# The run mask and the last factors of a graph network's last pass move to PSUM bank 7, its product groups to banks 0 to 6

## What is computed

```python
# he: edge_attr_16, rel_type: edge_type_90
V = weight.reshape(in_dim, num_bases, out_dim)
W_rel = jnp.matmul(w_comp, V).reshape(num_rels, in_dim, out_dim)
h_src = h[src]
z_src = h_src @ Ws.T
z_dst = h[dst] @ Ws.T
z_e = he @ Ws.T
e = jnp.concatenate([z_src, z_e, z_dst], axis=1) @ Wa.T
msg = jnp.einsum('ei,eio->eo', h_src, W_rel[rel_type]) * e
h_out = jax.ops.segment_sum(msg, dst, num_segments=n_nodes)
```

## Time and profile before

| what | value |
|---|---|
| median of 3 runs | 16045.7 us |
| lowest and highest | 16036.34 and 16046.12 us |
| span of the profiled execution | 16080.2 us |
| busy: PE, DVE, ACT, POOL | 77%, 79%, 50%, 74% |
| chain that ended last, by line | L637 on POOL 54% |
| mean granted clock of TensorE | 0.848 |

### The profile page before, as it was taken

How to read it: one execution, slowest core, us unless ns; L and a number is a source line. 1 busy time by engine, 2 the same in 40 slices (tenths; PEclk the granted TensorE clock), 3 DMA queues, 4 the chain that set the end, 5 groups by cost and what they waited for, 6 DMA issues and landing times.

```text
span 16080.2 us, 197886 instructions
## 1 busy us (share of the span) xinstructions
PE 12414.4 (77%) x62964; PEld 11204.4 (70%) x62964; DVE 12672.3 (79%) x13275; ACT 8008.6 (50%) x6941; POOL 11959.0 (74%) x12266
## 2 busy tenths in 40 slices
PE   6777777777599999599999488888888377777774
PEld 5555555555599998599999377777777376766764
DVE  7777777777577777477777589899989599999996
ACT  1111111111466666466666377777777255555552
POOL 6777777777777777677777677777777577777776
PEclk8888888888799999799999688898888577777776
DMA  1111111111122221122221122222222222222221
GB/s 37 28 27 27 28 28 27 28 28 26 33 40 39 40 39 37 28 40 39 40 39 38 37 48 50 50 51 50 50 47 48 44 61 62 63 60 63 61 62 37
DMA packets 811074, 675.53 MB, mean 42 GB/s; under 512 B 420924, under 2 KB 729500, under 8 KB 810500
## 3 DMA queue, kind: packets, MB, share of 16 engines
q1 hardware_dynamic: 419012, 545.90, 11.4%
q0 software_dynamic: 392000, 128.94, 9.3%
HBM read 507.78 MB, written 166.09 MB: 42 GB/s over the span
## 4 chain that ended last, share of the span: by engine, by line
POOL 57%; issue 20%; DVE 8%; DVEq 8%; PE 6%; DMA 1%; ACT 0%; POOLq 0%; SPq 0%; ACTq 0%
POOL deep L637 54%; DVE big L1292 6%; PE PS L855 5%; DVEq L1040 4%; DVEq L1297 3%; POOL deep L646 3%; DVE sml L1561 0%; DVEq L1232 0%; DVE acc L1229 0%; DMA wgt<-in_edge_weight 0%; DVEq L1286 0%; DVE sml L1553 0%; DVE acc L1566 0%; DVE sml L1554 0%; DVE sml L1558 0%
## 5 line engine op out<-in xcount | busy, mean ns | idle before, releaser
L637 POOL DMA_INDIRECT deep<-table,idx x11750 | 11475.0, 977 | 3824.8 <-issue 3579.0
L797 PE MATMUL PS<-tparts,hot 125*128 125x400 f32 x22000 | 4163.7, 350 | 482.7 <-DVE big L1451 305.4
L797 PEld LDWEIGHTS PS<-tparts,hot 125*128 125x128 f32 x22000 | 4078.7, 192 | 567.4 <-DVE big L1451 387.1
L1292 DVE TENSOR_TENSOR big<-PS,deep 128x768 f32<-128x768 f32 (+4 forms) x2750 | 2984.7, 1085 | 1082.2 <-DMA deep<-table,idx 515.5
L855 PE MATMUL PS<-tparts,rhot 125*128 125x426 f32 (+1 forms) x9000 | 2302.2, 428 | 527.7 <-DVE big L1292 293.8
L855 PEld LDWEIGHTS PS<-tparts,rhot 125*128 125x128 f32 x9000 | 2177.8, 246 | 616.3 <-DVE big L1292 320.7
L944 ACT ACTIVATE hot<-deep,ones_col 128x1536 fp32r<-128x1536 bf16 x1000 | 1447.6, 1472 | 1464.7 <-PE PS L797 1424.8
L754 PE MATMUL PS<-w0b_sb,big 128*128 128x256 f32 x6250 | 1826.1, 437 | 428.4 <-DVE big L1292 390.1
L754 PEld LDWEIGHTS PS<-w0b_sb,big 128*128 128x128 f32 x6250 | 1342.2, 222 | 933.7 <-DVE big L1292 475.0
L869 PE MATMUL PS<-wx,hot 115*128 115x272 f32 x12500 | 1726.1, 293 | 311.1 <-DVE big L1292 311.1
L1275 DVE TENSOR_REDUCE acc<-big 128x64 f32<-128x1024 f32 (+2 forms) x1875 | 1940.6, 1035 | 18.3
(11 more groups left out here) (281 smaller groups left out, 9713.7 us busy)
## 6 DMA issues: line engine op xcount, KB each, us to landing
wide<-edge_types SPq DMA_DIRECT2D x250, 800.0 KB, 6.1
deep<-table,idx POOLq DMA_INDIRECT x11750, 2.4
wide<-pick_codes SPq DMA_DIRECT2D x250, 352.0 KB, 3.5
running<-msg SPq DMA_DIRECT2D x250, 212.5 KB, 2.1
running<-msg SPq DMA_DIRECT2D x250, 200.0 KB, 2.0
running<-msg SPq DMA_DIRECT2D x125, 400.0 KB, 2.5
wide<-in_edge_attr SPq DMA_DIRECT2D x125, 200.0 KB, 2.5
tabo<-pick_codes SPq DMA_DIRECT2D x125, 160.0 KB, 4.6
```

The source lines that it names most:

```text
L637: pool.indirect_dma_start(g[:, j, 0:GW[l]], None, tab_dram[l][:, :], bass.IndirectOffsetOnAxis(ap=idx[:, s, j:j + 1], axis=0)).then_inc(ga ...
L797: last = pe.matmul(o, poneh[0:NQ, m, c], tparts[0:NQ, k, m * JC:m * JC + JC], start=m == 0 and k == 0, stop=m == BK - 1 and k == 1)
L1292: dve.tensor_tensor(products(j), matv(l, j, n), xs, ALU.mult).then_inc(mats_free, 1)
```

## The change

What the diff does:

- **Pass 4's mask** stands in PSUM bank 7 in f32, columns 0 to 415, as one buffer 16 features wide. Both scans read it there. ACT writes it (400 elements) when the scans of the chunk before are done (`scanned`); before, it asked for `chunks_done`. The zeros of its first column are written once ahead of the pass.
- **Pass 4's factor** goes to bank 7 as well (`fac_ps`, columns 420 to 444), and the multiplication that was L1650 reads it there. Since DVE now writes to bank 7 where ACT writes the mask, DVE waits for the mask (`masked`) ahead of the factor's sum and no longer ahead of the scans.
- **Pass 4's groups** get banks 0 to 6 alone: the three slots (4,3), (0,2), (2,2), then (4,2), (0,2), (2,2) and so on. Before, the groups stood at (0,3), (3,2), (5,2), (0,2), (2,2), (4,2), (6,2), (3,2), (7,1). Each group now waits for the group three before it. Before, that was 5, 3, 5, 3, 3, 3, 4, 2 and 2 before it, in the groups' order.
- **Passes 1 and 2**: ACT writes the mask of a chunk ahead of its one-hot vectors instead of behind them, and DVE waits for the mask at the chunk's start instead of ahead of the scan. Their scan goes over 442 elements instead of 416, because its length now comes from `FLATC`.
- A new event `banks_set` lets ACT start each of the passes 1, 2 and 4 only when DVE has set up bank 7.

```diff
-             [(0, 3), (3, 2), (5, 2), (0, 2), (2, 2), (4, 2), (6, 2), (3, 2), (7, 1)]]
+             [(4, 3), (0, 2), (2, 2), (4, 2), (0, 2), (2, 2), (4, 2), (0, 2), (2, 1)]]
...
-        def maskv(s):
-            return mask[:, HOME[s], :].rearrange("p (c t) -> p c t", t=CH + 1)
+        MASK_BANK = [[None] * 5] * 4 + [[7] * 5]
+        FLATC = [17, 17, 17, 17, 16]
+        def mask_flat(l, s):
+            n, b = FLATC[l] * (CH + 1), MASK_BANK[l][s]
+            return mask[:, HOME[s], 0:n] if b is None else PS[:, b, 0:n]
+        def maskv(l, s):
+            return mask_flat(l, s).rearrange("p (c t) -> p c t", t=CH + 1)
+        fac_ps = PS[:, 7, 420:420 + CH]
...
             def run_mask(l, it, s):
-                act.wait_ge(chunks_done, it * S + (NCH * l + s + S - 1))
-                act.activation(maskv(s)[:, :, 1:CH + 1], bc_r(same[:, bass.ds(it * (S * CH) + CH * s, CH)], 17),
+                if l == 4:
+                    act.wait_ge(scanned, it * S + (NCH + s))
+                else:
+                    act.wait_ge(chunks_done, it * S + (NCH * l + s + S - 1))
+                act.activation(maskv(l, s)[:, :, 1:CH + 1], bc_r(same[:, bass.ds(it * (S * CH) + CH * s, CH)], FLATC[l]),
                                ACT.Identity).then_inc(masked, 1)
...
                         act.wait_ge(rows_in[s], it * 16 + (row_base(l) + 16))
+                        run_mask(l, it, s)
                         code = rows_h[:, HOME[s], :]
...
-                        run_mask(l, it, s)
                         act.drain()
...
             def scans(l, it, s):
                 W = CW[l]
-                dve.wait_ge(masked, it * S + (NCH * l + s + 1))
-                for c0 in range(0, W, 17 if W == 17 else C):
-                    n = min(17 if W == 17 else C, W - c0) * (CH + 1)
-                    a = acc[:, HOME[s], c0 * (CH + 1):c0 * (CH + 1) + n]
-                    last = dve.tensor_tensor_scan(a, mask[:, HOME[s], 0:n], a, 0.0, ALU.mult, ALU.add)
+                if l in (0, 3):
+                    dve.wait_ge(masked, it * S + (NCH * l + s + 1))
+                n = FLATC[l] * (CH + 1)
+                for c0 in range(0, W * (CH + 1), n):
+                    a = acc[:, HOME[s], c0:c0 + n]
+                    last = dve.tensor_tensor_scan(a, mask_flat(l, s), a, 0.0, ALU.mult, ALU.add)
...
                         chunk_in(l, it, s)
-                        nodes_of_bank(l, it, s, iota_jr)
+                        dve.wait_ge(masked, it * S + (NCH * l + s + 1))
+                        nodes_of_bank(l, it, s, iota_jr(l, s))
...
             table_parts(4)
+            dve.memset(maskv(4, 0)[:, :, 0], 0.0)
+            dve.drain()
+            dve.sem_inc(ev["banks_set"], 1)
...
                         if i == 1:
-                            dve.tensor_tensor(sml[:, 1, :], term[:, s, :], gatv(s, 4)[:, :, C], ALU.add)
+                            dve.wait_ge(masked, it * S + (NCH * 4 + s + 1))
+                            dve.tensor_tensor(fac_ps, term[:, s, :], gatv(s, 4)[:, :, C], ALU.add)
                     matrices(4, it, s, C, whole_term)
-                    then(dve.tensor_tensor(m[:, :, 0:C], m[:, :, C:2 * C], bc_c(sml[:, 1, :]), ALU.mult))
+                    then(dve.tensor_tensor(m[:, :, 0:C], m[:, :, C:2 * C], bc_c(fac_ps), ALU.mult))
                     scans(4, it, s)
```

More of the change, by code:

```diff
@@ L46 @@
     "lp_tanh", "agg_n2", "agg_n",
-] + ["ln_in", "ln_out"] \
+] + ["ln_in", "ln_out", "banks_set"] \
   + ["tab", "strad_in", "strad_out", "strad_used", "out_ready"]
@@ L349, in accv, with iota_jr @@
             return acc[:, HOME[s], 0:CW[l] * (CH + 1)].rearrange("p (c t) -> p t c", t=CH + 1)
-        def maskv(s):
-            return mask[:, HOME[s], :].rearrange("p (c t) -> p c t", t=CH + 1)
+        MASK_BANK = [[None] * 5] * 4 + [[7] * 5]
[5 more added lines that the diff above has]
+            return mask_flat(l, s).rearrange("p (c t) -> p c t", t=CH + 1)
+        def iota_jr(l, s):
+            return iota_jr_ps if l in (1, 2) else iota_f[:, 0:JR]
+        iota_jr_ps = PS[:, 7, 512 - JR:512]
+        fac_ps = PS[:, 7, 420:420 + CH]
         def nodes(a, w=C):
@@ L365, in build_gnn @@
         iota_ps = PS[:, 7, P:2 * P]
-        iota_jr = PS[:, 7, 512 - JR:512]
         block = ctx.enter_context(nc.Block())
@@ L932, in pick_digits @@
                 y = PICKED.index(l)
+                act.wait_ge(ev["banks_set"], l)
                 with act.Fori(0, IT) as it:
@@ L1024, in _ @@
             root_of("ln_in", na[0:NQ, 3, :], na[0:NQ, 2, :], "ln_out", 3)
+            act.wait_ge(ev["banks_set"], 3)
             for s in range(S):
@@ L1437, in gcn_pass @@
                 y = PICKED.index(l)
-                then(dve.tensor_copy(iota_jr, iota_f[:, 0:JR]))
+                dve.tensor_copy(iota_jr_ps, iota_f[:, 0:JR])
+                dve.drain()
+                dve.sem_inc(ev["banks_set"], 1)
                 def pick_sum(s, i):
@@ L1459, in gcn_pass @@
                         columns_in(l, it, s, 0)
-                        then(dve.tensor_tensor(accv(s, l)[:, 1:CH + 1, :], gatv(s, l),
-                                               wgt[:, s, :].unsqueeze(2).to_broadcast([P, CH, C]), ALU.mult))
+                        then(dve.tensor_tensor(accv(s, l)[:, 1:CH + 1, :], gatv(s, l), bc_c(wgt[:, s, :]), ALU.mult))
                         scans(l, it, s)
@@ L1573, in hyper_chunk @@
                 chunk_in(3, it, s)
-                nodes_of_bank(3, it, s, iota_f[:, 0:JR])
+                nodes_of_bank(3, it, s, iota_jr(3, s))
                 matrices(3, it, s, 0, amid)
@@ L1641, in _ @@
                     chunk_in(4, it, s)
-                    nodes_of_bank(4, it, s, iota_f[:, 0:JR])
+                    nodes_of_bank(4, it, s, iota_jr(4, s))
                     sums_free(4, it, s)
```

## The result

| | median | runs |
|---|---|---|
| before | 16046.12 us | 7 (16036.34 to 16053.72) |
| changed | 16002.71 us | 7 (15995.96 to 16014.25) |
| ratio | 0.9973 | 95% interval 0.9962 to 0.9983 |

The change saves 43 us in this comparison; the interval reaches from 27 to 61 us. The forecast was 53 us less, 15993 us, with a range of 15972 to 16025.

What follows compares the result with a forecast made beforehand. POOL's source-row fetches, stretched by DVE in pass 4, were taken to bound the kernel, with DVE next. The terms 46.6 + 3.5 + 4 - 1 = 53 us, from 16045.7, gave 15993 us, range 15972 to 16025.

Steps and rivals of the forecast that it cites:

- The mechanism: Pass 4: DVE instructions with two SBUF inputs stretch POOL's fetches; one input in PSUM removes the stretch of 87.5 us.
- The rival in which the fetches are not freed: Pass 4: the scan's remaining SBUF accesses hold the lock, POOL stays at 25.74 us a chunk, time 16046; chance 0.07.
- The cap: Pass 4: of the 87.5 us stretch only the 46.6 us that DVE waits for fetched rows shows in the end.
- DVE's pace: Pass 4: DVE sets the pace once fetches are freed, at 25.31 us a chunk, above POOL's 25.03.
- The multiplication: Pass 4, L1650: 963 to 935 ns, 3.5 us gained; the mask's wait leaving the gap before the scan, 4 us.
- Scans from PSUM: Pass 4's scans reading f32 from PSUM cost 0 us, as PSUM is not dearer.
- The rival with the slower scan: Pass 4: each scan from PSUM takes 0.42 us more, DVE's pace is 26.16 us a chunk, time 16099; chance 0.07.
- the one with a dearer start: Pass 4: a PSUM input adds 0.07 us to each of three DVE instructions, 26 us lost, time 16019; chance 0.13.
- My own argument from L1254: L1254's 275 elements from PSUM (445 ns) and 125 from SBUF (292 ns) give 1.02 ns an element, 164 ns a start.
- The ring: Pass 4's new bank order: picks start some 0.6 us earlier; 0 us, with a gain of up to 7.3 us.
- Passes 1 and 2: ACT's `Abs` come 6.5 us later, covered by about 1.7 us: 0 us; the longer scan costs 1 us.
- The rival in which this comes too late: Passes 1 and 2: the `Abs` use up the cover; each further 0.2 us costs 50 us, time 16043; chance 0.04.

Runs made afterwards that it cites:

- each half alone: The changed kernel with only the scans reading PSUM (factor back in SBUF), or only the multiplication (mask back in SBUF): ratios to before 0.9966 and 0.9967.
- a_again: The changed kernel, unedited, timed and profiled once more beside the kernel before: 16001.97 us against 16052.72, ratio 0.9969.
- the second profile of before: The kernel before, unedited, profiled once more: span 16053.3 us; timed against itself, ratio 1.0.
- e2_factor_in_sbuf: The changed kernel with pass 4's factor back in SBUF, so only the scans read an input from PSUM: ratio to before 0.9966.
- e3_mask_in_sbuf: The changed kernel with pass 4's mask back in SBUF as bf16, so only the multiplication reads an input from PSUM: ratio to before 0.9967.
- the first experiment: The kernel before with only pass 4's groups moved to banks 0 to 6 in three slots, mask and factor staying in SBUF: ratio 1.0.

## Why the prediction was right, point by point

- **The mechanism.** Forecast: with one input in PSUM, the two scans and the multiplication no longer stretch fetches. Shown by the mean of 944 ns and by each half alone taking away half. The rival in which the fetches are not freed is out. More exactly than I wrote, only an instruction that is already running when the fetch starts holds it up.
- **The cap.** Forecast: only the 46.6 us that DVE waited show, not all of the stretch. Shown by those waits gone, by the two runs with more work on DVE (42 us on the changed kernel, none before), and by the one with less (46 us of 121).
- **DVE's pace.** Forecast 25.31 us a chunk. The copy's first and last start in the changed kernel (`a_again`) give (15834.3 - 12690.5) / 124 = 25.35, and in before (15889.7 - 12695.8) / 124 = 25.76. For pass 4 my terms made 54 us and my sign was 50 to 58 us; it is 49.9 and 49.8, just below that. The first pair of profiles, place by place on DVE over 124 chunks: 48.8 us less where it waited for fetched rows (forecast 46.6) and 5.7 less from the multiplication to the first scan (forecast 7.5), 2.5 less on its other instructions (forecast 0), but 4.6 more for the copy that POOL holds up and 2.8 more in front of the first pick, and neither of these was in my sum. So the 50 us are the forecast term with several small errors that partly cancel.
- **The multiplication.** It takes 946 ns now, where 963 was to become 935. Little of that is the factor's place: with the factor back in SBUF it takes 950, and in the second profile of before 953. The gaps ahead of the scans shrank from 12.8 to 9.2 us in the pass, close to the 4 us of the forecast. The rows are the multiplication with the factor in SBUF (`e2_factor_in_sbuf`), then the scans of pass 4 before:

```profile
L1676 DVE TENSOR_TENSOR acc<-acc,sml 128x400 f32<-128x400 f32 x125 | 118.7, 950 | 9.3
```

```profile
L1229 DVE TENSOR_TENSOR_SCAN acc<-mask,acc 128x416 f32<-128x416 bf16 x250 | 243.3, 1015 | 12.8
```

- **Scans from PSUM.** Forecast 0 us. The row by shape, DVE, whole span (before 1020 ns, which held scans of all three passes; L1676 is the old L1650):

```profile
L1249 DVE TENSOR_TENSOR_SCAN acc<-PS,acc 128x416 f32<-128x416 f32 x250 | 242.1, 1010 | 9.2
...
L1676 DVE TENSOR_TENSOR acc<-acc,PS 128x400 f32<-128x400 f32 x125 | 118.2, 946 | 9.3
```

With the mask in SBUF and all else as in the changed kernel (`e3_mask_in_sbuf`) the scan takes 1012 ns:

```profile
L1249 DVE TENSOR_TENSOR_SCAN acc<-mask,acc 128x416 f32<-128x416 bf16 x250 | 242.6, 1012 | 9.2
```

The rival with the slower scan is out, and so is the one with a dearer start. The 65 ns that are my estimate from the table of the Trainium skill ("VectorE: DVE Perf Modes", section "The TRN2 errata — SBUF-src ops pay a fixed extra latency per instruction") are not there: 1010 ns against 1012, and 946 against 950. My own argument from L1254 was weaker than it read, since its two rows differ in memory and in size at once. Two rows of `a_again` that both read PSUM give the split:

```profile
L1312 DVE TENSOR_TENSOR big<-PS,deep 128x1024 f32<-128x1024 f32 x750 | 917.3, 1223 | 93.7 <-issue 20.5
...
L1312 DVE TENSOR_TENSOR big<-PS,deep 128x256 f32<-128x256 f32 x125 | 53.1, 425 | 18.3
```

That is (1223 - 425) / 768 = 1.04 ns for each element and 159 ns for the start; the 125 elements from SBUF in 292 ns leave 162 at the same rate. So its conclusion holds.

- **The ring.** Forecast 0 us: shown by the first experiment. A step inside was off. I had the picks' 40 matmuls at 10.43 us at worst, and DVE's cover grow from 0.6 to 1.2 us. Now PE stands idle for 1.7 us in front of them, where it had no pause before, and they take longer, 422 ns each on average from 12700 to 15700 us instead of 415. One chunk of the changed kernel:

```profile
14025.72 0.80 PE L883 MATMUL PS<-w,hot 90*128 90x256 f32 x2 [0.42 <-DVE big L1312]
14028.22 10.89 PE L869 MATMUL PS<-tparts,rhot 125*128 125x426 f32 x40 [1.70 <-DVE big L1312]
```

They end at 14039.11, and DVE needed them at 14039.70, by the timeline: 0.6 us of cover as before. DVE's waits for picks went from 7.3 to 10.9 us, where I had allowed only for a gain. With the ring alone there is the same pause, 1.70 us, and the same 422 ns. Why each matmul takes longer is not shown.

- **Passes 1 and 2.** Forecast: `Abs` 6.5 us later, and covered. ACT in pass 1 now:

```profile
5000.49 0.56 ACT L906 ACTIVATE mask<-same 128x425 bf16 x1 [5.69 <-DVE msg L1257]
5000.95 5.54 ACT L957 ACTIVATE deep<-wide,negbank 128x1408 bf16<-128x1408 f16 x4
5006.64 5.56 ACT L963 ACTIVATE hot<-deep,ones_col 128x1536 fp32r<-128x1536 bf16 x4
```

The mask does wait for DVE's L1257, the end of the chunk two before, and the one-hot vectors follow without a wait for PE. DVE waits for PE no more than before, 317.9 us in pass 1 against 323.3. The rival in which this comes too late is out. What I had not seen is that DVE, which now asks for the mask at the chunk's start, waits for ACT there once in each turn of the loop:

```profile
DVE sel L1274 <- ACT mask L906: 29.0, 25, 8.0
```

It costs nothing, because DVE has room in these passes: its waits for fetched rows there are 96.6 us now and were 102.1.

- **The size.** The first comparison gave 43 us, the second 51, and the traces 50 in pass 4; the forecast of 53 lies within both intervals. Which of 43 and 51 is nearer can't be told from the runs, but pass 4's own 49.9 and 49.8 us speak for the second.

## What to carry to other kernels

When one engine limits a kernel and another stretches its work, compute the pace of both with and without the stretch before counting a gain: the smaller room decides, and here half of the edit was enough for all of it. A stretched instruction shows as a mean above the median with a long tail, and the culprit is what the other engine is already running when the stretched one starts. The place where the limiting engine has no one close behind it (here passes 1 and 2) is where the same edit pays in full.

## What the runs showed of the hardware that was not expected

- **The one that comes later gives way.** With one half of the change alone, a fetch of pass 4 that started while DVE ran a scan or multiplication with both inputs in SBUF ended 0.71 to 0.76 us after that instruction (247 of 248), and no fetch that had started before such an instruction was held up.
- **Who gives way changes sides.** With no instruction of DVE left that holds up a fetch, DVE's own small copy from SBUF to SBUF takes up to 419 instead of 200 ns, ending 20 to 30 ns after the fetch that it fell into; written as a reduction it takes 233 at most.
- **The stretch adapts.** With the unstretched fetch 3 ns quicker, POOL's busy time in pass 4 of before was the same (2456.4 and 2455.8 us), and 0.36 us more work for DVE in each chunk took the stretch from 983 to 976 ns a fetch. Before the change, the pace of 25.76 us thus seems to be set by both engines together, not by POOL's issue alone. That is read from these two cases and not tested; why it settles there is open.
- **Executions differ outside the changed pass.** Two profiles of the kernel before differ by 27 us, 26 of them in passes 0 to 3.
